# Two-part scores in pairs of heads, and the folding of the experts' matrices inside the images

## What is computed

```python
x = x + conv_attention(ln_c(x))          # layer norm over channels, then:
#   normed = group_norm(x, 32 groups) * gn_w + gn_b
#   q, k, v = split(qkv_w @ normed + qkv_b)        # 8 heads of 16 channels
#   weight = softmax((q * s)^T (k * s), over k's 1024 positions)
#   out = proj_w @ (normed_input + weight v) + proj_b
t = tokens(x)
t = t + moe(ln_t(t))                     # 8 experts, the best 2 of each token
#   h = x w1 + b1
#   y = (silu(h wg + bg) * (h wv + bv)) w2 + b2
```

## Time and profile before

| what | us |
|---|---|
| median of 3 runs | 2270.06 (2269.89 to 2271.42) |
| the profiled execution | 2275.42 |
| its span on the core | 2273.5 |
| normalize and project | 0 to 168.3 |
| attention: first maxima | 168.3 to 221.3 |
| image 0 | 221.3 to 320.2 |
| images 1 to 6 | 320.2 to 967.8, 107.9 each |
| image 7 | 967.8 to 1054.5 |
| the end: projection, plan, blanks, folding | to about 1142 |
| experts, second block | to 2273.5 |

### The profile page before, as it was taken

How to read it: one execution, slowest core, us unless ns; L and a number is a source line. 1 busy time by engine, 2 the same in 40 slices (tenths; PEclk the granted TensorE clock), 3 DMA queues, 4 the chain that set the end, 5 groups by cost and what they waited for, 6 DMA issues and landing times. The chain is left out here.

```text
span 2273.5 us, 41046 instructions
## 1 busy us (share of the span) xinstructions
PE 1929.1 (85%) x13306; PEld 1073.3 (47%) x13307; DVE 1436.2 (63%) x3154; ACT 1098.7 (48%) x1682; POOL 755.4 (33%) x883
## 2 busy tenths in 40 slices
PE   5769999999999999998589996996659992699993
PEld 2331223332332323232367774554447661599992
DVE  4769888888888888871346665762235665344444
ACT  4550665666666666666144442541225551344442
POOL 0232003343333333345335553000001667355551
PEclk9875999999999999999699998999879996799995
DMA  3851532323232323012333333322100242233326
GB/s 127 193 217 33 78 55 29 60 35 65 31 66 29 66 29 66 2 38 63 105 86 99 95 99 119 111 84 61 38 29 29 62 136 81 71 94 92 90 72 229
DMA packets 134782, 180.00 MB, mean 79 GB/s; under 512 B 44592, under 2 KB 87856, under 8 KB 132336
## 3 DMA queue, kind: packets, MB, share of 16 engines
q1 hardware_dynamic: 116208, 138.25, 25.6%
q0 software_dynamic: 18432, 39.88, 5.2%
HBM read 99.04 MB, written 69.01 MB: 74 GB/s over the span
## 5 line engine op out<-in xcount | busy, mean ns | idle before, releaser
L779 DVE TENSOR_REDUCE mx<-bank 128x1 f32<-128x512 f32 x1024 | 639.7, 696 | 86.4 <-PE bank L550 85.2
L726 ACT ACTIVATE P<-bank 128x1024 f32<-128x1024 f32 x512 | 497.4, 1021 | 313.1 <-PE bank L652 312.9
L550 PE MATMUL bank<-ks,qs 96*128 96x512 bf16 x1024 | 358.6, 402 | 35.5 <-DVE mx L779 35.5
L1290 POOL DMA_INDIRECT results<-yo,places x284 | 274.1, 965 | 283.6 <-DVE yo L1280 236.8
L652 PE MATMUL bank<-qs,ks 99*128 99x512 bf16 x1024 | 308.2, 384 | 2.6 <-ACT P L726 1.8
L1206 PE MATMUL bank<-xt,up 128*128 128x256 f32 x1136 | 274.8, 386 | 3.7 <-DVE xt L1257 1.4
L632 PE MATMUL bank<-P,vt 128*32 128x512 f32 x2048 | 272.8, 605 | 0.7 <-ACT P L726 0.7
L2289 POOL DMA_INDIRECT dispatched<-planes,places x128 | 124.5, 973 | 420.2 <-DVE stats L2133 357.3
L1206 PEld LDWEIGHTS bank<-xt,up 128*128 128x128 f32 x1136 | 207.5, 193 | 30.4 <-issue 4.7
L550 PEld LDWEIGHTS bank<-ks,qs 96*128 96x128 bf16 x1024 | 99.8, 98 | 257.5 <-DVE mx L779 177.7
L652 PEld LDWEIGHTS bank<-qs,ks 99*128 99x128 bf16 x1024 | 78.0, 97 | 280.0 <-ACT P L726 182.8
(11 more groups left out here) (298 smaller groups left out, 2581.8 us busy)
## 6 DMA issues: line engine op xcount, KB each, us to landing
xr<-dispatched SPq DMA_DIRECT2D x142, 130.0 KB
qk_parts<-parts SPq DMA_DIRECT2D x16, 768.0 KB, 5.1
qs<-qk_parts SPq DMA_DIRECT2D x84, 128.0 KB
ks<-qk_parts SPq DMA_DIRECT2D x84, 128.0 KB
v_turned<-vt SPq DMA_DIRECT2D x8, 1024.0 KB, 5.6
vt<-v_turned SPq DMA_DIRECT2D x8, 1024.0 KB
bands<-results SPq DMA_DIRECT2D x32, 256.0 KB, 3.7
y<-results SPq DMA_DIRECT2D x32, 256.0 KB
```

The lines of the kernel that those rows point to most:

```text
L550: pe.matmul(bank[:, slot, :], qs[par][0:KB, h, c * C:(c + 1) * C], ks[par][0:KB, h, half * HALF:(half + 1) * HALF], start=True, stop=True) ...
L726: act.activation(P[:, x % SLOTS, :], bank[:, 2 * pair:2 * pair + 2, :] .rearrange("p a t -> p (a t)"), ACT.Exp).then_inc(probs_ready, 1)
L779: dve.tensor_reduce(mx[:, k // 2, k % 2:k % 2 + 1], bank[:, slot, :], AX.X, ALU.max).then_inc(unit_freed, 1)
L1290: pool.indirect_dma_start(yd_dram, bass.IndirectOffsetOnAxis(places[:, p, q:q + 1], 0), yo[:, p, q, :], None).then_inc(sent[p], 16)
```

## The change

*Two parts.* q and k are split in two instead of three. The parts are 32-bit words, and casts and matmuls take them as `float32r` (F32R), a type for f32 values that were rounded; the cast to the first part rounds. Three of the four products are kept: 3 x 16 = 48 rows a head, and 2 rows for the maxima, 50 (KM). In normalize_and_project ScalarE casts once (`first_parts`) and VectorE (q) or GpSimd (k) subtracts once; the second cast and the last subtraction are gone. In the maxima's rows, `split_in_two` stands for `split_in_three`.

*Pairs.* Two heads share a tile: `stack_rows` puts the even head in partitions 0 to 49 and the odd one in 64 to 113, and `qs`, `ks` become [128, 4 pairs, 1024] in f32. Scores and maxima are matmuls over one half of the array's rows. The maxima are ordered so that neighbours are the two heads of one pair (`maximum`), two neighbours always stand in the same step (`BODY_GROUPS`), and where a step's units begin with a maximum, two stand behind its first pair of scores, else one (`first_half`). SP issues 24 stack loads an image as before, each for one half of a pair, and 4 rows of maxima instead of 3 per half of the heads. Ones are set in two memsets of [32, 4 x 1024] f32 per tile, those of `stacks0` already in the stage before.

*Folding.* The folding of an expert becomes three units of the images' list, `fold_turn`, `fold` and `fold_bias`, into the same three PSUM slots, and VectorE does the three copies. Images 1 to 6 fold expert b - 1 at about steps 21, 23 and 25; image 7 folds experts 6 (steps 11 to 15) and 7. SP loads the sources in two DMAs into tiles of their own behind the unit `("proj", 1)` of the image. In `last` nothing of the folding is left, and SP sends the blanks without a source between them.

```diff
-def split_in_three(eng, value, rest, parts, done, b, held=None):
+def split_in_two(eng, value, parts, done, b, held=None):
     if held is not None:
         eng.sem_inc(held, 1)
-    eng.tensor_copy(parts[:, 0], value).then_inc(done, 1)
-    eng.wait_ge(done, b * 4 + 1)
-    eng.tensor_tensor(rest, value, parts[:, 0], ALU.subtract).then_inc(done, 1)
...
+    eng.tensor_copy(parts[:, 0].bitcast(F32R), value).then_inc(done, 1)
+    eng.wait_ge(done, b * 2 + 1)
+    eng.tensor_tensor(parts[:, 1].bitcast(F32R), value, parts[:, 0], ALU.subtract).then_inc(done, 1)
+
+def stack_rows(u, r):
+    return slice(u * ROWS + r * CH, u * ROWS + (r + 1) * CH)
...
-                        sp.dma_start(stack[par][r * CH:(r + 1) * CH, 4 * g:4 * g + 4], src).then_inc(qk_loaded[g], 16)
+                        for u in range(2):
+                            sp.dma_start(stack[par][stack_rows(u, r), 2 * g:2 * g + 2], src[u]).then_inc(qk_loaded[g], 16)
...
-                    act.activation(parts[:, 1 - p, s, 1], rest[:, s], ACT.Copy).then_inc(second_parts, 1)
...
-            eng.tensor_tensor(parts[:, p, s, 2], rest[:, s], parts[:, p, s, 1], ALU.subtract).then_inc(split, 1)
+            eng.tensor_tensor(parts[:, p, s, 1].bitcast(F32R), qk[:, s], parts[:, p, s, 0], ALU.subtract).then_inc(ready, 1)
...
+    for step, k in ((11, 0), (21, 1)):
+        for n, kind in enumerate(("fold_turn", "fold", "fold_bias")):
+            at = (step + 2 * n) * len(units) // STEPS
...
+BODY_GROUPS = [unit for unit in BODY_UNITS if unit[0] != "max" or unit[1] % 2 == 0]
+STEP_OF = {unit: index * STEPS // len(BODY_GROUPS) for index, unit in enumerate(BODY_GROUPS)}
+STEP_OF.update({("max", k): STEP_OF["max", k - 1] for k in range(1, MAXIMA, 2)})
+
+def maximum(k):
+    pair, c, half, u = k // 32, k // 4 % TC, k // 2 % 2, k % 2
+    return pair, c, half, u
+
+def first_half(now):
+    return 2 if now and now[0][1][0] == "max" else 1
...
-                pe.matmul(bank[:, slot, :], qs[par][0:KB, h, c * C:(c + 1) * C],
-                          ks[par][0:KB, h, half * HALF:(half + 1) * HALF], start=True, stop=True).then_inc(unit_filled, 1)
+                pe.matmul(bank[:, slot, :], qs[par][rows, pair, c * C:(c + 1) * C].bitcast(F32R),
+                          ks[par][rows, pair, half * HALF:(half + 1) * HALF].bitcast(F32R), start=True, stop=True).then_inc(unit_filled, 1)
...
-            for e in range(1, 4):
-                load_source(e)
-            send_blanks(0)
-            load_source(4)
-            load_source(5)
-            send_blanks(1)
-            load_source(6)
-            load_source(7)
-            send_blanks(2)
-            send_blanks(3)
+            for part in range(4):
+                send_blanks(part)
...
-                            ins = pe.matmul(bank[:, 2 * pair + u, :], ks[par][:, head, s * C:(s + 1) * C],
-                                            qs[par][:, head, n * HALF:(n + 1) * HALF], start=True, stop=True)
+                            rows_of = slice(u * ROWS, u * ROWS + KM)
+                            ins = pe.matmul(bank[:, 2 * pair + u, :], ks[par][rows_of, 2 * g + pair, s * C:(s + 1) * C].bitcast(F32R),
+                                            qs[par][rows_of, 2 * g + pair, n * HALF:(n + 1) * HALF].bitcast(F32R), start=True, stop=True)
                         ins.then_inc(scores_ready, 1)
-                        for index, (kind, k) in now[:2] if pair == 0 else now[2:]:
+                        for index, (kind, k) in now[:first_half(now)] if pair == 0 else now[first_half(now):]:
...
+                            elif kind == "fold_turn":
+                                turn_w1(expert_of(before, k), slot)
+                            elif kind == "fold":
+                                multiply(expert_of(before, k), slot, base + units.index(("fold_turn", k)) + 1)
+                            elif kind == "fold_bias":
+                                sum_bias(expert_of(before, k), slot)
...
+            def copy_w1(e, slot, filled):
+                dve.wait_ge(unit_filled, filled)
+                dve.tensor_copy(wres[:, e, 4 * C:6 * C], bank[:, slot, 0:2 * C]).then_inc(unit_freed, 1)
...
-parts_dram = nc.dram_tensor("qk_parts", (B, 2, 3, C, T), BF16).ap()
+parts_dram = nc.dram_tensor("qk_parts", (B, 2, 2, C, T), F32).ap()
```

More of the change, by code:

```diff
@@ L295, in _ @@
         def _(pool):
+            for u in range(2):
+                pool.memset(stacks0[1][u * ROWS + 32:(u + 1) * ROWS], 1.0).then_inc(ones_set, 1)
+                pool.wait_ge(ones_set, u + 1)
             def step(db, b, nb, cb, p):
-                if db is not None:
-                    split_last(pool, 1, db, 1 - p, k_split)
                 if b is not None:
-                    split_rest(pool, 1, b, p, k_rest)
+                    split(pool, 1, b, p, k_split)
             over_images(pool, step)
@@ L347, in units_of @@
 def units_of(prev, more):
-    return [unit for unit in BODY_UNITS if (more or not of_next(unit)) and (prev or unit[0] in ("max", "rows"))]
+    return [unit for unit in BODY_UNITS if (more or not of_next(unit)) and (prev or unit[0] in ("max", "rows"))
+            and not (unit[0] in FOLDS and unit[1] == 0 and more)]
 FIRST_UNITS = [unit for unit in units_of(False, True) if of_next(unit)]
@@ L506, in body @@
                     load_v(b + 1, 1 - par)
+                units, base = units_of(prev, more), units_before(b) if prev else len(FIRST_UNITS)
+                if prev:
+                    load_source(b - 1, ("proj", 1), base, units)
                 max_rows(b, par, 1)
@@ L545, in take_max @@
             def take_max(b, par, k, slot):
[L547 removed]
+                pair, c, half, u = maximum(k)
+                rows = slice(u * ROWS, u * ROWS + KB)
                 if k % 64 == 0:
                     pe.wait_ge(qk_loaded[k // 64], b * LOADS)
[L550 to L551 removed]
+                pe.matmul(bank[:, slot, :], qs[par][rows, pair, c * C:(c + 1) * C].bitcast(F32R),
+                          ks[par][rows, pair, half * HALF:(half + 1) * HALF].bitcast(F32R), start=True, stop=True).then_inc(unit_filled, 1)
             def project(b, n, slot):
@@ L778, in reduce @@
                 dve.wait_ge(unit_filled, filled)
-                dve.tensor_reduce(mx[:, k // 2, k % 2:k % 2 + 1], bank[:, slot, :], AX.X, ALU.max).then_inc(unit_freed, 1)
+                pair, c, half, u = maximum(k)
+                row = 32 * (pair // 2) + 16 * u + 8 * (pair % 2) + c
+                dve.tensor_reduce(mx[:, row, half:half + 1], bank[:, slot, :], AX.X, ALU.max).then_inc(unit_freed, 1)
                 if k % 64 == 63:
@@ L821, in copy_ranks, with copy_product, add_bias @@
                 dve.tensor_copy(flat(ranked), bank[:, slot, 0:(G + 1) * E]).then_inc(unit_freed, 1)
+            def copy_w1(e, slot, filled):
+                dve.wait_ge(unit_filled, filled)
+                dve.tensor_copy(wres[:, e, 4 * C:6 * C], bank[:, slot, 0:2 * C]).then_inc(unit_freed, 1)
+            def copy_product(e, slot, filled):
+                dve.wait_ge(unit_filled, filled)
+                dve.tensor_copy(wres[:, e, 0:4 * C], bank[:, slot, :]).then_inc(unit_freed, 1)
+            def add_bias(e, slot, filled):
+                dve.wait_ge(unit_filled, filled)
+                dve.wait_ge(bias_loaded, 16)
+                dve.tensor_tensor(biases[:, e, :], bank[:, slot, 0:4], biases[:, e, :], ALU.add).then_inc(unit_freed, 1)
             def weigh_experts(then, b, copied):
@@ L903, in body @@
                             copy_logits(before, slot, filled)
+                        elif kind == "fold_turn":
+                            copy_w1(expert_of(before, k), slot, filled)
+                        elif kind == "fold":
+                            copy_product(expert_of(before, k), slot, filled)
+                        elif kind == "fold_bias":
+                            add_bias(expert_of(before, k), slot, filled)
                         else:
@@ L1052, in first @@
             def first():
-                for par in range(2):
-                    pool.memset(ks[par][KB:KM, :, :], 1.0).then_inc(ones_set, 1)
-                pool.wait_ge(ones_set, 2)
+                for u in range(2):
+                    pool.memset(ks[1][u * ROWS + 32:(u + 1) * ROWS], 1.0).then_inc(ones_set, 1)
+                    pool.wait_ge(ones_set, u + 1)
                 split_rows(0, 0, FIRST_UNITS.index(("rows", 0)) + 1)
```

195 lines of the change are left out of this document (70 added, 125 removed).

## The result

The changed kernel takes 2350.45 us in the median of four runs (2319.13 to 2378.73), against 2270.74 before (2269.89 to 2274.82). It is slower, and its runs scatter by 2.6% where those of before differ by 0.2%. The ratio 1.024 (95% interval 1.018 to 1.030) is that of the two lower runs of the four; whether the loss is over 2% it leaves open. The four times go with the mean granted clock: 2319.13 at 0.886, 2333.08 at 0.882, 2367.83 at 0.864, 2378.73 at 0.860. The profile is that of the run of 2367.83; the shortest of the four took 48.7 us less. Forecast were 2259 and a range of 2222 to 2340.

What follows compares the result with a forecast made beforehand. It took a loop of three PSUM slots that starves VectorE to bound the attention's steps. Stage 1 -14, start -3, images +19 and end -13 gave -11 us: 2264 profiled, 2259 as median; range 2222 to 2340.

Steps and rivals of the forecast that it cites:

- Stage 1: Normalize and project: fewer casts and subtractions, less 4 us for larger parts; -14 us, between -18 and +7.
- Start of the attention: VectorE's first copy waits for a memset that now writes half as many elements per partition; -3 us.
- The scores: Attention images: paired scores cost one 0.215 us stream, step of four falls to 2.71; net -3.6 us an image before costs.
- rivals 1 and 2: Scores: 1, wider type streams at f32 pace, about 2385 us; 2, pairs run one after another, 2300; chance 0.12 each.
- rival 2: Scores: pairs run one after another, loop keeps 2.93 us, images 1 to 7 about +8 each; 2300 us, chance 0.12.
- the loop: Attention step: fourth maximum waits for a PSUM slot, then weigh, scores and next maximum, while VectorE starves 0.53 us.
- I take 2: Scores and maxima: slower weight load of the wider type, partly hidden; +2 us an image, between 0 and 5.3.
- the uneven steps: Attention images: maxima placed by twos give steps of four, six or two; a step of two about 0.2 us worse.
- Folding in the images: Expert folding moved into the images' steps, not hidden in TensorE's slack; +4.0 us an image, at most 4.0 + 1.2.
- The end: End of the attention: blanks sent without sources save 17.5 us, lower clock returns 4.5; -13 us, between -6 and -18.
- rival 3: Attention images: TensorE's clock falls as its streams shrink, a third of steps at 1.2 GHz; 2370 us, chance 0.05.

Runs made afterwards that it cites:

- the run with half-sized parts: Changed kernel with q and k parts and stacks in bf16, third part left out, and folding back at the end: 2233.85 us, ratio 0.983.
- the run with the same half of the rows: Changed kernel with folding back at the end and neighbouring scores and maxima taken from one half of the array's rows: 2453.37 us, ratio 1.077.

## Why the prediction was wrong

*Stage 1* (-14, between -18 and +7): -20.3, beyond its bound. The two parts that it counted were right (L232 gone, L255 at 0.22), and it left out L285, which GpSimd's second subtraction had stretched from 0.81 to 2.51: 1.7 an image, partly given back by a longer split (2.46 for L224, 1.21 for L227). The bytes probably cost more than the 4 that it took: the run with half-sized parts ends this stage 14 us earlier, and its period is only 0.2 us shorter.

*Start of the attention* (-3): -3.4. VectorE's first copy takes 3.46 instead of 6.88, as elements per partition gave it.

*The scores.* One stream of the new type costs nearly a bf16 stream (0.24 from pair to pair, in bf16 0.22), and a pair costs one: both right, so rivals 1 and 2 fell, though what rival 2 said of the loop, that it keeps its 2.93, came true by another cause. The price that failed is "I take 2" for the weight load, between 0 and 5.3 an image: 0.24 a step, the difference to the run in bf16, is 6.7 over 28 steps, beyond the upper end. The step of four stayed at 2.94 instead of 2.71. With the uneven steps the pairs cost 1.4 an image at full clock where -1.1 was the sum of the forecast. The rule of the Trainium skill, "TensorE: Matmul & The Clock Gate", Weight-path perf modes, gives the fast load to 128 weights of every type but FP32; here the rounded 32-bit type loads in 0.2 us, like f32, and not like bf16.

*Folding in the images* (+4.0): 4.5 alone and at most 5.5 beside the pairs (114.8 less 109.3). It was right that TensorE's slack would not hide it. What the forecast left out is that its one-column products are places at which the clock falls.

*The end* (-13, between -6 and -18): -19.7, beyond its bound. Without the sources the blanks gave 19.9 instead of 17.5 (from the plan to the experts' first load 24.6 us, before 44.5), and the 4.5 that the clock was to take back did not come: the plan is ready 45.4 us behind the last scores (1215.82), before 45.3.

*The clock* is the step that failed: the sum has every image but the first steps of image 0 at full clock. In the profiled run the lower clock costs 83 us, against a net loss of 92; without it, by this estimate, the kernel would have been some 9 us slower than before and within the range. The forecast had it as rival 3, at 2370 and a chance of 0.05, on the argument that TensorE "stayed at 1.00 in the image 7 window without maxima". Only the second half of that window has no maxima (VectorE is busy 34.4 us in the first half and 8.0 in the second). There TensorE was busy 94% and kept its clock, with scores over 99 rows beside weigh's f32 streams: this shows that it may be idle a little more, and nothing of matmuls over half of the rows among maxima that wait for VectorE. Image 7 of the changed kernel keeps 1.00 throughout, too; the loss lies in the images before it, which have maxima in nearly every step.

The forecast counted streams in time, 1.7 of 2.71 us, and the runs with fewer rows show that time busy is not the measure: TensorE is busy 98% in them and they lose the clock. Two scores over 48 rows side by side fill as many rows as one over 96 does, for half as long; that this is why the pairs lose the clock is argued, not shown. Rival 3's size was met closely, in part by luck: it took a third of the steps at the lower clock and 14 us an image, and images 1 to 6 of the profiled run spend 256 of 772 us at it and lose 13.9 each. The four runs take from 2319 to 2379.

The range fits its terms badly as well: their bounds, added up straight, give about 2210 to 2320 and not 2225 to 2292.

What stays open is why the same waits and short products cost the clock in one kernel and not in the other, and why, in one kernel, they do so in one image and not in the next; and whether the clock in the changed kernel could be kept by other work in its gaps, which was not tried.

## What to carry to other kernels

Ahead of a change that shortens matmuls in rows, or runs small ones side by side in less time, look at the granted clock of the stretch: the saving is in streams, and the loss of the clock falls on all that TensorE does there. Where one engine starves in a loop of few slots, first try the order of issue: moving one group of matmuls ahead of the one that waits was worth 1.3% in the unchanged kernel and 1.8% on top of the bf16 pairs, without a byte more. Work that is moved into a loop of that kind may be paid in full, however much idle time its engines show: here 4.5 us an image for 4.0 us of TensorE's work.

## What the runs showed of the hardware that was not expected

Fewer rows at work went with a lower granted clock. With the same instructions over 96 to 99, 64 to 67 and 32 to 35 rows it was 1.00 in all, 0.63 to 1.00 and 0.62 to 0.63 in the image windows shown. In between it has two ways: with 64 rows the same image's work took 113.0 us at 1.00 or 165.9 at 0.63, in one execution. That the changed kernel's runs scatter by 2.6% for the same reason is likely, and not shown.

Two matmuls in different halves of the array's rows run side by side even if they are not neighbours in the program: in the run with the same half of the rows, scores of the second half start 0.014 us behind those of the first, ahead of the maxima that stand between them. To part two streams it was not enough to issue others between them.

With 67 and 64 rows in turn the step at full clock is 3.14 us, 0.2 longer than with 99 and 96, though nothing else is changed. The trace has it between the two kinds: from the last of two scores to the first maximum, or back, are 0.31 us (median in an image at full clock), before 0.215, while two of the same kind follow in 0.22 to 0.23 in both. So a change between these two heights costs 0.1 us.
